# First products of the MLP and the centre product in rounded passes, and moved to other places of a pipelined step

## The reference

```
x = x + attn_a(layernorm(x))          # softmax attention, 16 heads of 8
x = x + ffn(layernorm(x))             # first call
x = x + attn_b(layernorm(x))          # linear attention (elu + 1), 16 heads of 8
x = x + ffn(layernorm(x))             # second call

def ffn(x):                           # two layers, each:
    h = shift_token(x)                # second half of the features one token later
    q, k, v = split(h @ wqkv)         # 8 heads of 64
    q, k = l2norm(q) * qs, l2norm(k) * ks, then rotary with xpos scales
    x = x + local_attention(q, k, v) @ wo      # windows of 64, one window back
    h = shift_token(x)
    h = (h - mean(h)) / sqrt(var(h) + 1e-5) * lg + lb
    a, g = split(h @ w1 + b1)         # w1: 128 x 682
    x = x + (a * gelu(g)) @ w2 + b2   # w2: 341 x 128
```

## Time and profile before

| what | value |
|---|---|
| median of 3 runs | 1079.81 us (1075.5 to 1079.89) |
| profiled execution, its own time | 1079.84 us |
| its span, first to last instruction | 1078.1 us |
| mean granted TensorE clock | 0.955 |
| start of `stream` on PE | 304.2 us |
| plain cycle, steps 14 to 17 (438.75 to 480.80) | 10.36 + 9.08 + 13.11 + 9.50 us |
| cycle with b, steps 29 to 32 (609.09 to 667.51) | 13.43 + 13.67 + 12.39 + 18.93 us |

### The profile page before, as it was taken

One profiled execution on the slowest core, in us unless ns is written; L12 is line 12 of the kernel. 1 busy time (PEld: TensorE's weight loads), 2 busy tenths in 40 slices (PEclk: granted clock), 3 DMA queues, 4 the chain that ended last, 5 costly groups with the idle time before them and its releaser, 6 DMA issues.

```text
span 1078.1 us, 21971 instructions
## 1 busy us (share of the span) xinstructions
PE 1006.5 (93%) x8314; PEld 602.4 (56%) x8314; DVE 735.5 (68%) x1202; ACT 736.6 (68%) x1565; POOL 385.3 (36%) x269
## 2 busy tenths in 40 slices
PE   6999999999978999999999898989899999999986
PEld 3433433333346666766766566656666766766752
DVE  3777755775458786777877676666777777777741
ACT  2276755765858778788787676666858778788762
POOL 2102003000056654644644342434344644634410
PEclk9899966997989999999999998999999999999997
DMA  2200000000032110101110000000000110111100
GB/s 66 64 14 2 2 1 0 3 1 1 1 66 65 31 26 17 31 16 27 23 25 21 17 20 6 21 16 20 17 21 17 31 23 20 31 26 26 31 21 10
DMA packets 25219, 23.66 MB, mean 22 GB/s; under 512 B 10610, under 2 KB 17052, under 8 KB 25116
## 3 DMA queue, kind: packets, MB, share of 16 engines
q1 hardware_dynamic: 25116, 22.27, 8.8%
HBM read 6.16 MB, written 1.05 MB: 7 GB/s over the span
## 4 chain that ended last, share of the span: by engine, by line
PE 58%; DVE 8%; ACT 2%; issue 2%; POOL 1%; DVEq 0%; POOLq 0%
PE psum L1273 8%; PE psum L1242 5%; PE psum L1182 5%; PE psum L1203 5%; PE psum L1144 5%; PE psum L1154 4%; PE psum L1192 4%; PE psum L1281 4%; PE psum L1146 4%; PE psum L1145 4%; PE psum L1266 2%; PE psum L1215 2%; PE psum L1260 2%; PE psum L1167 2%; DVE f_PT L1536 2%
## 5 line engine op out<-in xcount | busy, mean ns | idle before, releaser
L1073 POOL TENSOR_TENSOR f_A<-f_A,f_BS 128x1024 f32<-128x1024 f32 x64 | 150.8, 2357 | 221.1 <-DVE f_BS L1512 220.8
L755 DVE TENSOR_REDUCE a_M<-psum 128x2 f32<-128x1024 f32 x128 | 156.4, 1222 | 71.4 <-PE psum L560 70.5
L687 ACT ACTIVATE a_PT<-psum 128x1024 f32<-128x1024 f32 x128 | 130.1, 1019 | 59.0 <-PE psum L570 58.4
L1078 POOL TENSOR_TENSOR f_A<-f_A,f_RN 128x1024 f32<-128x1024 f32 x64 | 121.7, 1902 | 90.9 <-ACT f_RN L1404 86.9
L1389 ACT ACTIVATE f_PW<-psum,f_NM 128x128 f32<-128x128 f32 x512 | 138.0, 380 | 4.2 <-DVE f_NM L1544 4.2
L1544 DVE TENSOR_REDUCE f_NM<-psum 128x4 f32<-128x512 f32 x128 | 82.3, 684 | 66.0 <-PE psum L1182 64.8
L1355 ACT ACTIVATE f_SQ<-psum 128x512 f32<-128x512 f32 x128 | 75.1, 608 | 70.0 <-PE psum L1146 65.4
L1508 DVE TENSOR_TENSOR f_A<-psum,cos 128x512 f32<-128x512 f32 x128 | 87.7, 685 | 44.2 <-ACT f_SQ L1355 44.1
L1203 PE MATMUL psum<-f_VS,f_PT 128*64 128x65 f32 x1024 | 80.5, 227 | 32.6 <-DVE f_hidden L1591 13.8
L1203 PEld LDWEIGHTS psum<-f_VS,f_PT 128*64 128x64 f32 x1024 | 67.3, 138 | 65.6 <-issue 48.3
L1273 PE MATMUL psum<-f_mid,f_w 128*128 128x512 f32 (+1 forms) x192 | 87.7, 607 | 2.7 <-DVE f_mid L1574 2.7
(11 more groups left out here) (189 smaller groups left out, 2012.9 us busy)
## 6 DMA issues: line engine op xcount, KB each, us to landing
f_VS<-f_V SPq DMA_DIRECT2D x112, 130.0 KB, 2.3
raw<-L_ffn_wqkv_dram SPq DMA_DIRECT2D x2, 768.0 KB, 5.3
a_XT<-L_attn_a_x_dram SPq DMA_DIRECT2D x4, 256.0 KB, 2.9
a_QS<-a_MROW SPq DMA_DIRECT2D x64, 2.0 KB, 1.7
out_dram<-f_OUT SPq DMA_DIRECT2D x4, 256.0 KB, 2.3
f_w<-L_ffn_w_dram SPq DMA_DIRECT2D x2, 341.0 KB
tables<-const_dram SPq DMA_DIRECT2D x1, 512.0 KB, 4.1
f_wo<-L_ffn_wo_dram SPq DMA_DIRECT2D x8, 64.0 KB
```

The costliest lines, as they stand in the source:

```text
L687: nc.scalar.activation(PT[:, h:h + 2, t, :], psum[:, pair("by_key", i), :], ACT.Exp, scale=float(DA) ** -0.5).then_inc(s("exped"), 1)
L755: nc.vector.tensor_reduce(M[:, quads % 2, t, 2 * j:2 * j + 2], psum[:, pair("scores", i), :], AX_X, ALU.max).then_inc(s("maxed"), 1)
L1073: nc.gpsimd.tensor_tensor(A[:, k % 2, :, :], A[:, k % 2, :, :], BS[:, k % 2, :, :], ALU.add)\
L1078: nc.gpsimd.tensor_tensor(x, x, RN[:, k % 2, :, None].to_broadcast([P, 2 * HW, DW]), ALU.mult)\
```

## The change

Five things change, all in `stream` and its table:

- `turn_p_2` stands directly behind `turn_p` on PE, ahead of the scores (before: behind them), and on DVE ahead of the maxima.
- `w1` moves from the middle of its step to the end of it, on PE, ACT and DVE; its DVE part is no longer split in two.
- `w1` and `center_mlp` run in rounded passes. `w1_h` and `w1_l` are made once, in two early steps, by ACT and POOL (`split_w`); the split of the second projection weights moves four steps back to make room. `mid` becomes a high and a low part: POOL writes both for the centre product (two copies, one copy of zeros, two subtractions), DVE both behind the norm (one operation more).
- To make room in SBUF, tiles share memory: `LR` is `ln_squared`, `hidden` is `gates` (which holds `w1` at first), `NEGK` is `KB`, and `LAT`, `OB`, `OF` and `OUT` lie in other tiles. Waits are adapted to this.
- The waits of the first products go with the banks that the new order gives them.

```diff
 STEP = {
     "PE": [...
-           ("turn_o", 3, of_tile), ("w1", 5, of_group), ("turn_p", 2, of_tile),
+           ("turn_o", 3, of_tile), ("turn_p", 2, of_tile), ("turn_p_2", 2, of_tile),
...
-           ("var_y", 10, of_sequence), ("turn_p_2", 2, of_tile), ("w2", 6, of_group), ("wo", 3, of_group), ("sums", 2, of_tile), ("store", 6, of_end)],
+           ("var_y", 10, of_sequence), ("w2", 6, of_group), ("wo", 3, of_group), ("sums", 2, of_tile),
+           ("w1", 5, of_group), ("store", 6, of_end)],
...
     "POOL": 
+    ... ("split", 8, of_tile), ("scale", 0, of_tile), ("split_w", 0, of_weights), ...
...
+                        for half, (rows, to, of) in enumerate(SHIFTED):
+                            nc.gpsimd.tensor_copy(mid_h[rows, to], Y[rows, n, of]).then_inc(s("shifted_mid"), 1)
...
+                        for half, (rows, to, of) in enumerate(SHIFTED):
+                            nc.gpsimd.tensor_tensor(mid_l[rows, to], Y[rows, n, of], mid_h[rows, to].bitcast(F32),
+                                                    ALU.subtract).then_inc(s("low_mid"), 1)
...
+                            nc.tensor.matmul(dst, center_r[:, :], mid_h[:, :], start=True, stop=False)
+                            pe.wait_ge(s("low_mid"), 2 * j + 2)
+                            nc.tensor.matmul(dst, center_r[:, :], mid_l[:, :], start=False, stop=True)\
+                              .then_inc(s("center"), 1)
...
+                                nc.tensor.matmul(dst, w1_h[:, layer, of], mid_h[:, :], start=True, stop=False)
+                                nc.tensor.matmul(dst, w1_l[:, layer, of], mid_h[:, :], start=False, stop=False)
+                                nc.tensor.matmul(dst, w1_h[:, layer, of], mid_l[:, :], start=False, stop=True)\
+                                  .then_inc(s(kind), 1)
...
-                            nc.vector.tensor_scalar(mid[:, :], mid[:, :], vecs[:, layer, 1:2], None, ALU.add)\
-                              .then_inc(s("ln_done"), 1)
+                            nc.vector.tensor_scalar(mid_h[:, :], LR[:, :], vecs[:, layer, 1:2], None, ALU.add)\
+                              .then_inc(s("ln_high"), 1)
+                            dve.wait_ge(s("ln_high"), j + 1)
+                            nc.vector.scalar_tensor_tensor(out=mid_l[:, :], in0=LR[:, :],
+                                                           scalar=vecs[:, layer, 1:2], in1=mid_h[:, :].bitcast(F32),
+                                                           op0=ALU.add, op1=ALU.subtract).then_inc(s("ln_done"), 1)
```

More of the change, by code:

```diff
@@ L1272, in _ @@
                             for kind, first in (("gate", HID), ("up", 0)):
-                                nc.tensor.matmul(take(kind, 3 * i + blk)[0:w, :],
-                                                 w1[:, layer, first + lo:first + lo + w],
-                                                 mid[:, :], start=True, stop=True).then_inc(s(kind), 1)
+                                dst = take(kind, 3 * i + blk)[0:w, :]
+                                of = slice(first + lo, first + lo + w)
+                                nc.tensor.matmul(dst, w1_h[:, layer, of], mid_h[:, :], start=True, stop=False)
+                                nc.tensor.matmul(dst, w1_l[:, layer, of], mid_h[:, :], start=False, stop=False)
+                                nc.tensor.matmul(dst, w1_h[:, layer, of], mid_l[:, :], start=False, stop=True)\
+                                  .then_inc(s(kind), 1)
                     elif stage == "w2":
@@ L1427, in _ @@
                           .then_inc(s("weights_high"), 1)
+                    elif stage == "split_w":
+                        act.wait_ge(s("weights"), 16 * len(weights))
+                        if i % 2 == 1:
+                            nc.scalar.activation(w1_h[:, i // 2, :], w1[:, i // 2, :], ACT.Copy).then_inc(s("w1_high"), 1)
                     elif stage[:7] == "center_":
@@ L1569, in _ @@
                             layer = j // SEQS % LAYERS
-                            nc.vector.scalar_tensor_tensor(out=mid[:, :], in0=x, scalar=vecs[:, layer, 0:1],
+                            nc.vector.scalar_tensor_tensor(out=LR[:, :], in0=x, scalar=vecs[:, layer, 0:1],
                                                            in1=LR[:, :], op0=ALU.mult, op1=ALU.mult)\
@@ L1582, in _ @@
                             nc.vector.tensor_tensor(Y[:, j, :], x, LR[:, :], ALU.mult).then_inc(s("ln_used"), 1)
-                    elif stage in ("w1", "w1_last"):
+                    elif stage == "w1":
                         layer = i // SEQS % LAYERS
-                        for blk in (0, 1) if stage == "w1" else (2,):
+                        for blk in range(3):
                             w = HID_BLOCKS[blk][1]
```

92 lines of the change are left out of this document (55 added, 37 removed).

## The result

| | before | after |
|---|---|---|
| median of 20 runs each | 1080.08 us | 1071.80 us (1052.75 to 1083.93) |
| profiled execution: time, span, granted clock | 1079.84, 1078.1, 0.955 | 1063.99, 1061.9, 0.963 |
| steps 1 to 12 | 111.53 us | 109.97 us |
| a plain cycle / a cycle with b | 42.05 / 58.4 | 42.55 / 54.4 |
| step 13 to the start of step 64 | 604.16 us | 593.33 us |

The account below looks back on a forecast made before the run. PE was taken to set the pace, busy 1006.5 of 1078.1 us. 1079.84 + 0.5 (plain cycles) - 16 (b cycles) - 1 (start and end) = 1063.3, stated as 1063.5 us; 8-in-10 range 1040 to 1080.

Parts of the forecast that it names:

- start and end: Steps before and after the repeating cycles: -1 us together, bounds -4 and +4.
- Passes: MLP's first products: 5.15 us to some 4.3; centre product: 1.02 to 0.55-0.6; some 1.25 us freed a cycle.
- Both turns in front: Ahead of the scores: 13.2 us of waits on second turned weights go; PE waits for k's bank instead.
- The walk through the cycle: Plain cycle's four steps: 8.3 + 12.7 + 10.6 + 10.5 = 42.1 us, against 42.05 before.
- The plain cycles' sum: Ten plain cycles: 2.95 us freed, 3.0 given back in each, +0.5 in all; bounds -29 and +12.
- The b cycles: Four cycles carrying attention b: 7 us freed, 3.1 given back, taken as -4 each, -16 in all; bounds -28 and 0.
- POOL: Two more subtractions for `mid`, 2.45 us: hidden in the stream with 0.8 to spare, +2.0 at the end.
- 1 (stalls bind little): Waits ahead of the scores bind little, as ACT and DVE run further ahead: about 1036 us; chance 0.13.
- 2 (b cycles as long as ever): b's tokens and centre of y wait as long as the removed waits: no change, 1079 us; chance 0.17.
- 3 (the clock falls behind the new stalls): Granted clock drops behind 28 new stalls in plain and b cycles: slower, 1098.5 us with all; chance 0.11.
- 4 (exposed loads): Each new pass pays its weight load, 20 a group of 0.188 us: +60, 1123.5 us; chance 0.02.

Follow-up runs that it names:

- experiment 3: Changed kernel with the projection in the order q, v, k, so the mask product's second half takes v's bank; median 1063.88 us, ratio 0.966 to the kernel before.
- experiment 4: Changed kernel with only the second turn of weights put back behind the variance; median 1065.55 us, ratio 0.969 to the kernel before.
- Experiment 5: Changed kernel with DVE's third operation behind MLP's norm left out, or done twice; traces only: plain cycle 42.10 or 43.33 us, b cycle 53.65 or 55.21.
- experiment 1: Changed kernel's order, but MLP's first products and the centre product in fp32; median 1067.36 us, ratio 0.974 to the kernel before.
- experiment 6: Rounded passes throughout, the changed order only in the four steps with b's tokens, elsewhere the order of before; median 1057.60 us, ratio 0.975 to the kernel before.
- Experiments 2: Rounded passes in the order of the kernel before; median 1057.74 us, ratio 0.972 to the kernel before.

## Why the prediction was right, and where it was not

The forecast of 1063.5 us stands against a median of 1071.80 and a profiled 1063.99. That agreement in the profiled execution is partly luck: 3.75 of its 16.2 us fell before the stream starts (304.60 before, 300.85 after), in code that is the same in both. From step 1 on the change saves 12.4 us, and I had said 16.5. Of the 4.1 that are missing, 3.2 lie in the plain cycles and 1.5 in the b cycles; start and end gave 0.6 more than said.

**Passes: right.** 18 passes in 4.29 us (4.3 said), the centre product's two in 0.64 (449.38 to 450.02; 0.55 to 0.6 said). A weight load of L1307 takes 198 ns on 128 columns, about what one of the projection's takes, and 18 loads stand within 4.29 us of passes 0.234 apart. By the Trainium skill's rule, "TensorE: Matmul & The Clock Gate", Part 3, loads that go to the same rows of the array would not overlap; here they do. (The same part lets loads into a background buffer of weights go ahead as well; no run here tells the two apart.)

**Both turns in front: right in mechanism and nearly in size.** The wait for the second turned weights went, PE waits for `k`'s bank, and experiment 3 moved the wait by moving the bank. The walk through the cycle:

| step | said | measured |
|---|---|---|
| centre | 8.3 | 8.29 |
| first products | 12.7, stall 1.6 partly ahead of the turn of `o` | 12.70, 1.17 and some 0.3 there |
| `w2` | 10.6, stall 1.2 | 10.66, stall 1.15 |
| `wo` | 10.7 in layer 0, else 10.3 | 10.91, else 10.38 (behind a `w2` step of 11.07) |

**The plain cycles' sum was mis-sized.** I had +0.5 us for all of them; steps 13 to 24 and 45 to 63 give +3.7: +3.0 from six cycles of layer 0, nothing from the one whole cycle of layer 1, and +0.8 from steps 61 to 63, which lack the centre step, where the new order gains. In layer 0 a cycle takes 42.55 where the walk gives 42.3, six times: its `wo` step has the stall (0.43) but loses 0.53 by it (10.91 against the 10.38 of a step without), and `w2` 0.06. And I set the mean of both layers against a cycle of layer 0: in the other, the cycle of before takes 42.45, and the change's 42.44, since its `w2` step is 0.4 longer than in layer 0, which I had not walked.

**The b cycles: right in size, wrong in place.** 54.4 against 54.5 said, -14.5 us in steps 25 to 44 where I had -16. I put one stall of 2.5 us ahead of b's tokens. It is two:

```profile
587.29 0.47 PE L1167 MATMUL psum<-f_qkv_h,HH 128*128 128x512 f32 x1 [1.24 <-DVE f_ln_squared L1610]
...
593.89 1.22 PE L1348 MATMUL psum<-f_CTX,f_BQ 128*128 128x144 f32 x8 [1.09 <-issue]
...
609.26 0.70 PE L1290 MATMUL psum<-X,const 128*128 128x512 f32 x1 [1.68 <-DVE X L1711]
```

1.24 us already stand at the start of the step: with the banks moved on by the turn, `q`'s bank is that of the centre product of the step before, free after DVE's first norm operation. The 5.1 us of waits on `mid` that I had counted as freed came back there as 4.9, under another name. In experiment 4, with the turn back behind the variance, this wait stands at the sums again, 5.1 in all. Then 1.09 ahead of the tokens, not 2.5: DVE's masked context started at 593.49 and took 0.30 (the earlier trace rows before), so it was done at 593.79, and the tokens start at 593.89; the word "issue" there hides a wait for data. (It is not the bank: in experiment 3, with `v`'s bank, the wait stayed at 4.4 us in all.) Experiment 5 bears this out: a longer chain on DVE lengthens this wait by 0.8 us, and the profile then names the context. The step that failed is the one that took PE to be undelayed up to the tokens. The wait for `X` ahead of y's centre product is 1.68, 6.8 in all; the same product waited 1.9 in all before, so +1.2 a cycle where I had 0.6. Given back by this: 1.24 + 1.09 + 1.2 = 3.5, said 3.1.

**POOL: right; start and end: near, and loosely measured.** In the stream POOL's low part was there at 448.91, 0.78 us ahead of the pass that reads it (449.69), as said (0.8). At the end PE waits 2.37 and 2.00 us for POOL and 3.58 for DVE's norm, and still the end is no longer than before: -0.06 in all. With the order alone (experiment 1) it took 55.85, so the order gains here and the passes, with what they ask of POOL and DVE, cost as much; how much of it is the clock is not worked out. Steps 1 to 12 gave -1.56, but the same kernel once more took 110.91 there, which is -0.62. I had -1 for both.

**The rivals.** 1 (stalls bind little): no, 31.3 us of them. 2 (b cycles as long as ever): no, -4 each. 3 (the clock falls behind the new stalls): not in the changed kernel, whose cycles show 1.00 behind every one of these waits. But it is no fancy: in one of the four b cycles of experiment 6, after a wait of 2.13 us for `X`, the granted clock was 0.56 over the next 3.9 us, mostly the lower of its two levels, and that step took 16.11 us in place of 14.50. The other three had the same wait (2.12 to 2.14 us) and a clock of 1.00 behind it, so the wait alone does not decide; what does is open. 4 (exposed loads): no, as above.

**What I did not see** is the price of having all in one order. The new order pays in the b cycles, where it keeps PE from waiting 3.45 us for `hidden`; in the plain cycles it costs 0.5 and takes away the 1.35 that the passes give in the order of before. Experiments 2 and 4 part its two moves: with the passes, moving the first products costs 0.76 us a plain cycle (40.70 to 41.46) and gains 2.3 in a b cycle (57.73 to 55.43), and the turn in front then costs 1.09 and gains 1.0. The walk said as much, with 2.95 freed and 3.0 given back, but I asked only what the whole would do, not which part was throwing away the gain of the other.

## What to carry to other kernels

When work moves off a path that an in-order engine sets, ask next which buffer its neighbours now get: here two turns in front turned a free bank (`q`) into a late one (`k`), and the projection's products in another order bought 1 us a cycle back. Faster work is worth its time only where its engine is not waiting; measure a speed-up in each of the orders before both are joined, and let an order hold only in the steps where it pays. And walk a whole cycle with its durations: the lengths of the steps came out to 0.2 us, while the places of the stalls needed the banks as well.

## What was not expected of the hardware

The stretch ahead of the stream, the same code in all these kernels, took from 297.6 to 318.4 us. Its granted clock went with it: 0.92 in the shortest (experiment 6), 0.86 in the longest (experiment 3). This alone spreads the runs by 2%, more than most of the edits here are worth, while a plain cycle of the stream repeats to 0.05 us.

```profile
0.00:297.50 297.50, 279.43 (x1435) 108.98 (x1436) 186.92 (x226) 178.08 (x222) 36.34 (x45) 0.92 0.05 14
```

```profile
0.00:318.00 318.00, 299.48 (x1432) 112.04 (x1433) 187.15 (x226) 178.27 (x222) 35.66 (x44) 0.86 0.05 13
```

DVE and ACT are busy for the same 187 and 178 us in both; PE alone takes longer for its products (299 us against 279).
